# One-core attention and expert kernel: column-block matmuls, and another order of work behind the last scores

## What is computed

```python
Q, K, V = x @ wq, x @ wk, x @ wv                    # 16 heads of 8
local = window_attention(Q, K, V)                   # window of 32 rows
GQ = x @ wgq; GK, GV = pool8(x @ wgk), pool8(x @ wgv)   # 8 latent heads of 8, 64 latents a sequence
rem = (causal softmax(GQ GK^T) GV) @ r_out_w
att = (sigmoid(Q . gate_local_w) * local + sigmoid(Q . gate_remote_w) * rem) @ w_out
x = layernorm(x + att)
h = int(x[:, 0] + x[:, 1]) mod 8                    # experts h and h + 1 (mod 8), each weighted 1/2
y = sum over the two experts of 0.5 * (relu(x @ W1[e] + b1[e]) @ W2[e] + b2[e])
out = layernorm(x + y)
```

## Time and profile before

| | |
|---|---|
| median of 3 runs | 242.28 us (241.79 to 242.59) |
| profiled execution, its own time | 243.42 us |
| its span in the trace | 241.4 us |
| TensorE busy | 216.1 us, 90% |
| VectorE busy | 151.5 us, 63% |
| ScalarE busy | 121.5 us, 50% |
| POOL busy | 117.3 us, 49% |
| granted TensorE clock, mean | 0.958 of 2.4 GHz |

### The profile page before, as it was taken

How to read it: one execution, slowest core, us unless ns; L and a number is a source line. 1 busy time by engine, 2 the same in 40 slices (tenths; PEclk the granted TensorE clock), 3 DMA queues, 4 the chain that set the end, 5 groups by cost and what they waited for, 6 DMA issues and landing times.

```text
span 241.4 us, 9967 instructions
## 1 busy us (share of the span) xinstructions
PE 216.1 (90%) x3623; PEld 182.5 (76%) x3623; DVE 151.5 (63%) x523; ACT 121.5 (50%) x360; POOL 117.3 (49%) x218
## 2 busy tenths in 40 slices
PE   7979998999999999998996899897999999999930
PEld 3545777877888678886874599886899999999920
DVE  7835457795877867888898525374556656555640
ACT  3534656665577646765754246652434353434410
POOL 6453034661744428662747330648465465545541
PEclk9988999999999999999999569999999999999995
DMA  3231130032212233120001435412112112111100
GB/s 98 57 93 45 48 91 3 3 92 90 89 33 80 72 101 92 45 69 15 27 25 44 124 110 175 133 35 66 45 49 49 54 51 55 30 38 44 34 22 7
DMA packets 18553, 14.68 MB, mean 61 GB/s; under 512 B 2646, under 2 KB 15546, under 8 KB 18512
## 3 DMA queue, kind: packets, MB, share of 16 engines
q1 hardware_dynamic: 17008, 11.83, 17.5%
q0 software_dynamic: 1216, 2.16, 2.7%
q10 hardware_dynamic: 288, 0.13, 0.2%
HBM read 11.43 MB, written 3.03 MB: 60 GB/s over the span
## 4 chain that ended last, share of the span: by engine, by line
PE 64%; DVE 11%; issue 9%; DMA 6%; ACT 3%; POOL 2%; DVEq 2%; POOLq 1%; ACTq 0%
PE bS L1295 9%; PE bT L1244 7%; DMA out<-yo,idx 5%; PE bV L1435 4%; PE bV L1428 4%; PE bS L1187 4%; PE bV L1259 3%; PE bS L1212 3%; PE bV L1266 3%; PE bJ L1163 3%; PE bS L1226 2%; PE bL L1347 2%; PE bT L1295 2%; PE bS L1194 2%; PE bL L1361 2%
## 5 line engine op out<-in xcount | busy, mean ns | idle before, releaser
L681 ACT ACTIVATE ha<-bS,b1c 128x128 f32<-128x128 f32 x68 | 19.4, 368 | 40.0 <-PE bS L1295 40.0
L669 ACT COPY PTs<-bT 128x512 f32<-128x512 f32 (+3 forms) x48 | 25.8, 538 | 19.4 <-PE bT L1244 19.3
L568 POOL DMA_INDIRECT out<-yo,idx x18 | 19.2, 1067 | 17.8 <-POOL idx L564 9.8
L1244 PE MATMUL bT<-ident,Pr 128*128 128x128 f32 x168 | 27.4, 282 | 0.1
L1295 PE MATMUL bS<-xsT,w_s 128*128 128x128 f32 x204 | 26.4, 279 | 0.9 <-issue 0.8
L499 POOL TENSOR_SCALAR rstd<-mv 128x1 f32<-128x1 f32 x16 | 3.8, 235 | 45.7 <-DVE mv L860 45.7
L1295 PEld LDWEIGHTS bS<-xsT,w_s 128*128 128x128 f32 x204 | 24.1, 192 | 2.1 <-issue 2.1
L1244 PEld LDWEIGHTS bT<-ident,Pr 128*128 128x128 f32 x168 | 20.5, 147 | 4.1 <-issue 3.8
L515 POOL DMA_INDIRECT groups<-x,pos x16 | 16.6, 1035 | 12.5 <-DVE pos L910 9.1
L815 DVE TENSOR_REDUCE mx<-bS 128x8 bf16<-128x512 f32 x32 | 21.4, 676 | 0.0
L656 ACT ACTIVATE Pr<-bS 128x512 f32<-128x512 f32 x32 | 19.9, 622 | 2.6 <-PE bS L1226 2.6
(11 more groups left out here) (236 smaller groups left out, 515.5 us busy)
## 6 DMA issues: line engine op xcount, KB each, us to landing
w_s<-in_L_ffn_W SPq DMA_DIRECT2D x16, 256.0 KB
w1f<-in_L_ffn_W SPq DMA_DIRECT2D x10, 256.0 KB, 2.7
xrow<-groups SPq DMA_DIRECT2D x22, 64.5 KB, 1.8
xs<-groups SPq DMA_DIRECT2D x18, 64.0 KB
x_tok<-in_L_attn_x SPq DMA_DIRECT2D x4, 256.0 KB, 3.2
groups<-padrows SPq DMA_DIRECT2D x1, 516.0 KB, 5.7
b2r<-in_L_ffn_b SPq DMA_DIRECT2D x1, 512.0 KB, 3.7
out<-yo,idx POOLq DMA_INDIRECT x18
```

Source lines behind the costliest of these rows:

```text
L568: nc.gpsimd.indirect_dma_start(rows_out, bass.IndirectOffsetOnAxis(ap=idx[:], axis=0), yo[:, FULL - 1, :], None, bounds_check=T * P - 1, o ...
L669: nc.scalar.copy(PTs[:, j, 0:m, :], bT[:, 0:m * P].rearrange("p (c q) -> p c q", c=m)).then_inc(turned_out, 1)
L681: nc.scalar.activation(dst[:, c, :], src[:, c * P:(c + 1) * P], ACT.Relu, bias=bias_of(c)).then_inc(relu, 1)
L1244: last = nc.tensor.transpose(bT[:, c * P:(c + 1) * P], Pr[:, t % 2, j, c * P:(c + 1) * P], ident[:])
```

## The change

VectorE: residual(t - 3) moves ahead of the tile table in round T, and full_biases behind gate. The table loses two instructions (two steps made one by a constant that POOL prepares at the start; one cast for both rows of full_table), and a third (taken) moves behind the last mark. The five registers are read in three places: two ahead of gate(15), two ahead of residual(15), one behind the last mark. TensorE: weigh's latent part and fill "G" go by blocks of 32 weight columns into the four (for wgk two) quarters of the partitions; columns(0) moves from round T + 1 to the head of round T + 2; rank_last moves from j = 1, behind up_full(2, 0), to j = 0, behind up_full(1, 1). SyncE: one semaphore for each weight buffer instead of one for all, so that a load no longer waits for the one before it; weights 1 and 2 are asked for right behind the rows of tiles 0 and 1. ScalarE copies half the partitions of GKs.

```diff
@@ constants on POOL
+                link(nc.gpsimd.tensor_scalar(tile_scale[:], efl[:, 0:E], -1.0 / P, 0.5 / P - 0.5, ALU.mult, ALU.add))
@@ SyncE
             def load_full_weights(j):
-                if j >= 1:
-                    sp.wait_ge(w1f_in, 32 * j)
                 if j >= WR:
                     sp.wait_ge(up_b, j - WR + 1)
                 for s in range(2):
                     sp.dma_start(w1f[:, j % WR, s, :].unsqueeze(1),
-                                 W1[bass.ds((experts[j] + s) % E, 1)].rearrange("e p f -> p e f")).then_inc(w1f_in, 16)
+                                 W1[bass.ds((experts[j] + s) % E, 1)].rearrange("e p f -> p e f")).then_inc(w1f_in[j % WR], 16)
...
                 sp.dma_start(xrow[:, j * XW:(j + 1) * XW], seg[bass.ds(rows[j], P), :]).then_inc(full_in[j], 16)
-            for j in range(1, FULL):
+                if 1 <= j + 1 < WR:
+                    experts += load_table(sp, full_table[:, 0, :], [j + 1], full_ok, E - 1)
+                    load_full_weights(j + 1)
+            for j in range(WR, FULL):
                 experts += load_table(sp, full_table[:, 0, :], [j], full_ok, E - 1)
-                if j < WR:
-                    load_full_weights(j)
-            for j in range(WR, FULL):
                 load_full_weights(j)
@@ ScalarE
-                    nc.scalar.mul(GKs[:, q, :], src[:, 0:NL], 1.0 / CH)
+                    nc.scalar.mul(GKs[0:LD, q, :], src[0:LD, 0:NL], 1.0 / CH)
@@ VectorE
-                link(nc.vector.tensor_tensor(m[:, Z + 1:], nextrow[:], efl[:, 0:E], ALU.subtract))
-                link(nc.vector.tensor_scalar(m[:, Z + 1:], m[:, Z + 1:], 1.0 / P, 0.5 / P - 0.5, ALU.mult, ALU.add))
+                link(nc.vector.scalar_tensor_tensor(m[:, Z + 1:], nextrow[:], 1.0 / P, tile_scale[:], ALU.mult, ALU.add))
...
+                return upto
+
+            def take_tiles(upto):
                 link(nc.vector.tensor_tensor(taken[:], upto[:, Z + 1:], upto[:, Z:Z + E], ALU.subtract))
-                return upto
...
-                link(nc.vector.tensor_copy(full_table[:, 0, :], expert_of[0:1, :]))
-                nc.vector.tensor_copy(full_table[:, 1, :], rowf[0:1, :]).then_inc(full_ok, 1)
+                nc.vector.tensor_copy(full_table[:], found[0:1, :, :]).then_inc(full_ok, 1)
@@ VectorE, the loop over t
+                if t < T:
+                    largest(t, 2)
+                    largest(t, 0)
+                if t == T + 2:
+                    experts += load_table(dve, full_table[:, 0, :], [2, 3], full_ok, E - 1)
+                if t >= 3:
+                    residual(t - 3)
                 if t == T:
                     upto = full_tiles()
                     full_rows(upto)
-                if t < T:
-                    largest(t, 2)
-                    largest(t, 0)
-                if t >= 3:
-                    residual(t - 3)
+                if t == T + 1:
+                    experts = load_table(dve, full_table[:, 0, :], [0, 1], full_ok, E - 1)
...
+                if 2 <= t < T + 2:
+                    gate(t - 2)
                 if t == T:
                     full_biases()
-                if 2 <= t < T + 2:
-                    gate(t - 2)
...
             mark(NB - 1)
+            take_tiles(upto)
+            experts += load_table(dve, full_table[:, 0, :], [4], full_ok, E - 1)
             place(NB - 1)
             count_tiles()
-
-            experts = load_table(dve, full_table[:, 0, :], range(FULL), full_ok, E - 1)
@@ TensorE, fill "G"
-                    mm(dst[:, 0:NL], wgk_s[:], xp[:, q, :], start=True, stop=True)
+                    for i in range(LD // W):
+                        mm(dst[i * W:(i + 1) * W, 0:NL], wgk_s[:, i * W:(i + 1) * W], xp[:, q, :], start=True, stop=True)
 
                     for m in range(KT_):
-                        last = mm(dst[:, NL + m * LD:NL + (m + 1) * LD],
-                           xph[:, m, :, :].rearrange("p h l -> p (h l)"), wgv_s[:], start=True, stop=True)
+                        for i in range(BLK):
+                            last = mm(dst[i * W:(i + 1) * W, NL + m * LD:NL + (m + 1) * LD],
+                                      xph[:, m, :, :].rearrange("p h l -> p (h l)")[:, i * W:(i + 1) * W], wgv_s[:],
+                                      start=True, stop=True)
@@ TensorE, weigh, j == 2
                     for c in range(k + 1):
-                        last = mm(bV[:, HP * PW:(HP + LP) * PW], PTs[:, j, c, :],
-                                  GVx[:, b % 2, c, :, :].rearrange("p a w -> p (a w)"), start=(c == 0), stop=(c == k))
+                        for i in range(BLK):
+                            last = mm(bV[i * W:(i + 1) * W, HP * PW:(HP + LP) * PW], PTs[:, j, c, i * W:(i + 1) * W],
+                                      GVx[:, b % 2, c, :, :].rearrange("p a w -> p (a w)"), start=(c == 0),
+                                      stop=(c == k), skip_group_check=True)
@@ TensorE, up_full
-                    pe.wait_ge(w1f_in, 32 * (j + 1))
+                    pe.wait_ge(w1f_in[j % WR], 32 * (j // WR + 1))
@@ TensorE, the loop over t
                 if t == T + 2:
+                    columns(0)
                     up_full(0, 0)
...
-                if t == T + 1:
-                    columns(0)
@@ TensorE, the loop over full tiles
-                if j == 1:
-                    rank_last()
                 if j == 3:
                     more_tiles([2, 3])
                 down_full(j, 1)
                 if j + 1 < FULL:
                     up_full(j + 1, 1)
+                if j == 0:
+                    rank_last()
```

More of the change, by code:

```diff
@@ L141, in bass_windowed_latent_attention_hash_moe @@
         reached = sb("reached", [P, FULL, E])
-        expert_of = sb("expert_of", [P, FULL])
         cover = sb("cover", [P, FULL, E])
         gone = sb("gone", [P, FULL])
-        rowf = sb("rowf", [P, FULL])
         chosen = sb("chosen", [P, FULL, E])
@@ L150, in bass_windowed_latent_attention_hash_moe @@
         full_table = sb("full_table", [1, 2, FULL], I32)
+        tile_scale = sb("tile_scale", [P, E])
+        found = sb("found", [P, 2, FULL])
         w1_s = sb("w1_s", [P, E, F])
@@ L231, in bass_windowed_latent_attention_hash_moe @@
         scattered_late = sem("scattered_late")
-        w1f_in = sem("w1f_in")
+        w1f_in = [sem(f"w1f_in{j}") for j in range(WR)]
         full_ok = sem("full_ok")
@@ L937, in full_rows @@
                                              jrow[:, 0, :].unsqueeze(2).to_broadcast([P, FULL, E]), ALU.is_le))
-                nc.vector.tensor_reduce(expert_of[:], reached[:], AX.X, ALU.add)
+                nc.vector.tensor_reduce(found[:, 0, :], reached[:], AX.X, ALU.add)
                 link(nc.vector.tensor_tensor(cover[:], reached[:], ends, ALU.mult))
                 link(nc.vector.tensor_reduce(gone[:], cover[:], AX.X, ALU.max))
-                link(nc.vector.scalar_tensor_tensor(rowf[:], gone[:], -float(P), jrow[:, 1, :], ALU.mult, ALU.add))
-                link(nc.vector.scalar_tensor_tensor(rowf[:], expert_of[:], float(SEG), rowf[:], ALU.mult, ALU.add))
-                link(nc.vector.tensor_copy(full_table[:, 0, :], expert_of[0:1, :]))
-                nc.vector.tensor_copy(full_table[:, 1, :], rowf[0:1, :]).then_inc(full_ok, 1)
+                link(nc.vector.scalar_tensor_tensor(found[:, 1, :], gone[:], -float(P), jrow[:, 1, :], ALU.mult, ALU.add))
+                link(nc.vector.scalar_tensor_tensor(found[:, 1, :], found[:, 0, :], float(SEG), found[:, 1, :],
+                                                    ALU.mult, ALU.add))
+                nc.vector.tensor_copy(full_table[:], found[0:1, :, :]).then_inc(full_ok, 1)
             def full_biases():
                 dve.wait_ge(b1d_ok, 1)
-                link(nc.vector.tensor_tensor(chosen[:], expert_of[:].unsqueeze(2).to_broadcast([P, FULL, E]),
+                link(nc.vector.tensor_tensor(chosen[:], found[:, 0, :].unsqueeze(2).to_broadcast([P, FULL, E]),
                                              efl[:, 2 * E:].unsqueeze(1).to_broadcast([P, FULL, E]), ALU.is_equal))
```

## The result

The changed kernel takes 241.89 us (median of 20 runs, 239.09 to 245.10); the kernel before, beside it on the same chip, 243.32 us (20 runs, 241.79 to 244.66). The ratio is 0.9921, with a 95% interval of 0.9896 to 0.9947: faster by 0.8%, 1.4 us by the medians and 1.9 us by the ratio. The prediction asked for 5.35 us and its range ended at 239.6, so it was wrong. The profiled execution is a lucky one, at 239.59 us with a span of 237.9: 2.3 us under its own median, where that of before stood 1.14 over the median of the three runs known then and 0.10 over that of the 20. The two spans differ by 3.5 us, about twice what the change is worth.

What follows compares the result with a forecast made beforehand. The prediction took the chain as nearly two thirds TensorE, with VectorE stretches and late stores. Its terms, 2.5 + 1.0 - 0.75 + 0.6 + 2.0 = 5.35 us, came off 242.28 for 236.9 us, range 235.0 to 239.6.

Steps and rivals of the forecast that it cites:

- Part 1: Attention tiles: 32-column blocks in weigh latent and fill G shorten TensorE's groups, 2.5 us gain, bounds 0.5 to 3.5.
- (a): Attention tiles: VectorE's maxima and ScalarE's exponentials are the cycle, so column blocks give only 0.5 us, 238.9 us; chance 0.17.
- Parts 2 and 3: Behind the last scores: residual ahead of the table, columns(0) one step later; wO ends 1.0 us earlier, bounds 0 to 2.9.
- Part 4: Before the small tiles: rank_last one tile earlier makes TensorE stand for the ranks, -0.75 us; place comes 1.6 us earlier.
- Part 5: SyncE's weight loads: a semaphore for each buffer means weight 3 no longer comes late, 0.6 us gain.
- Part 6: First small expert tiles: VectorE's earlier register reads bring sums and stores forward, hb stall goes; 2.0 us, bounds 0 to 2.65.
- (b): Behind the last scores: the gains are eaten, all but the column blocks give 0.8 us together, 239.0 us; chance 0.13.
- (c): From 134 to 142 us: TensorE keeps 2.4 GHz, 1.9 us more gain, 235.0 us; chance 0.10.
- (d): Column blocks: 32-column weight loads don't overlap, so the kernel gets slower, 22 us slower at 0.11 us a load; chance 0.03.

Runs made afterwards that it cites:

- after: The changed kernel, with column blocks and new order, against the kernel before: 241.89 us, ratio 0.9921.
- blocks_only: The kernel before with the 32-column blocks alone (weigh latent, fill G, GKs copy): 243.13 us, ratio 1.0009 to the kernel before.
- order_gblocks: The changed kernel with only fill G's column blocks kept, weigh's latent part undone: 250.63 us on a slower chip, ratio 1.0101 to the kernel before.
- o_columns_back: The changed kernel without column blocks and with columns(0) back in round T + 1: 239.46 us, ratio 0.9842 to the kernel before.
- order_only: The changed kernel with the column blocks undone (full 128-column weights again): 239.31 us, ratio 0.9851 to the kernel before.
- o_weights_back: The changed kernel without column blocks and with SyncE's old order and waits for rows and weights: 239.55 us, ratio 0.9837 to the kernel before.
- before: The kernel without the change, run beside the others: 243.32 us beside the changed kernel, 242.86 to 249.27 us in the follow-up batches.
- before_spread: The kernel before with each round's second expert weight load (W2) sent half a round later: 242.77 us, ratio 0.9982 to the kernel before.
- o_regs_back: The changed kernel without column blocks and with VectorE's five register reads back in one piece: 240.53 us, ratio 0.9911 to the kernel before.
- o_rank_back: The changed kernel without column blocks and with rank_last back at j = 1: 238.60 us, ratio 0.9783 to the kernel before.
- after_spread: The changed kernel with each round's second expert weight load (W2) sent half a round later: 240.57 us, ratio 0.9877 to the kernel before.
- before_again: The kernel before, unchanged, run for a second trace on a slower chip: 247.95 us.
- after_again: The changed kernel, unchanged, run for a second trace on a slower chip: 247.81 us.
- after2: The changed kernel, unchanged, run again on a fourth, slow chip: 246.51 us, ratio 0.9888 to the kernel before.
- order_only2: The changed kernel without column blocks, run again on a fourth, slow chip: 247.87 us, ratio 0.9994 to the kernel before.

## Why the prediction was wrong, step by step

**Part 1, column blocks: 2.5 us forecast, none in the runs. This is the step that failed.** The prices were near in sum: a latent pass takes 0.51 / 24 = 0.021 us and not 0.016, so a latent block gains some 0.05 us ((0.85 - 0.64) / 4) and not 0.085, and a G gains 0.55 and not 0.45. The same count, 20 blocks and four Gs, comes to 3.2 us by these, against 3.5. What failed is "what TensorE saves there arrives, as long as VectorE and ScalarE keep up". It has two faults. First, less is saved than the count says: TensorE is busy only 1.1 us less, some 1.5 us arrive in traces with equal stalls, and 0.97 of 1.8 between tiles 4 and 12. Rival (a) had looked for this loss in VectorE's and ScalarE's pace. It is there once, as the 0.50 us behind the second G, but their waits don't grow in sum, and where the rest goes stays open.

The second fault is in no rival: TensorE's idle time grows by 1.4 us, and its "issue" stalls go from 1.26 to 3.17 us. The change adds 344 matmuls to TensorE's program, and the instruction stream is itself loaded, three transfers more (30 against 27). That the stalls are late instructions, the traces bear out; that the added matmuls make more of them is argued from `after` and `blocks_only` and not shown, since kernels without blocks had stalls of 1.01 and 0.99 us and `order_gblocks` had the most. The trace of before had such stalls in plain sight, 0.65, 0.19 and 0.23 us in TensorE's groups at 37.95, 52.21 and 67.67 us, if only as a small part of the 9% "issue" of the chain; I never asked what they were. What makes the runs of 242 to 245 us, of which no trace exists, is not shown either. Their mean granted clock is lower (0.950 in the two slowest, 0.970 and 0.973 in the two fastest), as in the longer runs of before, and whether a stall or the clock comes first can't be told without their traces.

**Parts 2 and 3, 1.0 us forecast, 0.1 to 0.3 in the traces.** With the lead of 1.33 us added, the table came at 132.6 us (132.6 forecast), SyncE asked for xrow(0) at 135.4 (135.4 forecast), columns(0) began at 137.7 (137.4) and up_full(0, 0) at 138.6 (138.0). Two terms were too small. xrow(0) needed 2.25 us to land behind two weight loads and not the median of 1.8, and the transpose, the copy and the hand-overs took 0.9 us and not 0.6. And at the low clock (0.55 and 0.60 from 136 to 144 us) the two up groups with aT between and wO needed 4.4 us and not 4.2. What the earlier trace rows showed as 1.56 us idle was slack of the last tile's chain for the most part: the next residual took its place with 1.18 us. `o_columns_back` shows no gain of part 3.

**Part 4, -0.75 forecast.** TensorE stands 0.23 us there in `order_only`; the stage is 0.4 to 0.5 shorter without the move, and the runs on the 243 us chips lean the same way (0.9783 against 0.9851, on different chips), those on the slow one the other (1.0003 against 0.9968, with intervals that overlap). Sign right on the one sort of chip, size some 0.5, and the gain it was made for stays unproved.

**Part 5, 0.6 forecast, 0 in the stage and 0.2 in the runs.** The weight is no longer late, but the 0.86 us wait of `o_weights_back` does not lengthen the stage. The ranks' wait and the clock hide it in that trace, so the worth of this part stays open.

**Part 6, 2.0 forecast, 1.9 to 2.04.** Right in its sum, a little late in its steps: measured from the first small tile, the wait for the fourth store ends 5.79 us behind it and not 7.37, where 2.3 us were to be gained and 1.6 were. The 1.23 us wait for hb is gone, and 0.73 us are left for ysum at 167.22 (0.6 forecast). The registers alone are 1.0 to 1.1 of it in the stage and 1.2 in the runs. No run takes the rest apart; the earlier start of place and scatter is my guess.

Parts 2 to 6 together were to give 2.85 us. `order_only` gave 3.6 by its ratio on one chip and 0.1 to 0.8 us on the slow one, and 2.3 in its trace on the first. So their sum came about right there, but nearly all that a trace shows of it is part 6; parts 2 to 5 were to give 0.85 and give next to nothing.

**The rivals.** (b) was wrong on the first chip: parts 2 to 5 lost their gain where it looked, but with part 6 they gave 2.3 us in the traces and not 0.8. On the slow chips it describes what came. (c) did not come: the clock fell later (1.00 in 132 to 136 us, where it was 0.54) and stayed low up to wO. (d) is false: 32-column weights with all 128 rows follow each other at 0.021 us a pass. The rule of the Trainium skill (TensorE: Matmul & The Clock Gate, "Packing small matmuls — row/col tiling") that the row group must differ for a load to overlap isn't what these rows show.

**The starting point.** I took the sum off the median of three runs, 242.28 us, where 20 gave 243.32, and read it from a profile of before at the low clock from 16 to 20 us. That belongs to the execution, not to the kernel, and made the comparison of two profiles look 1.5 us better than the runs.

## What to carry to other kernels

Cutting matmuls into more, smaller ones may be paid for in instructions: before counting on it, sum TensorE's idle time with "issue" as its releaser and see whether groups are cut in their middle near large transfers. Take a wait from one trace as a price only after asking what is late next; of four such waits here only one gave a gain that can be told, the registers in front of the sums, and that was 1.2 us where 1.7 to 2 were expected. And align two traces at a landmark ahead of the change before their spans are compared.

## What the runs showed of the hardware

- TensorE's "issue" stalls of 0.15 us or more between 20 and 130 us end 1.2 to 1.6 us behind an instruction transfer, in all 41 cases on the chips where before takes 243 us. Beside two loads of 256 KB they reach 1.94 us, behind 4 MB 3.47 us; with the DMA engines nearly idle there are stalls too, up to 2.57 us.
- In the stretch from 16 to 20 us the granted clock is 0.57 in the profiles of `before`, `before_spread`, `o_regs_back` and `o_weights_back` and 1.00 in `after`, `order_only`, `blocks_only`, `o_rank_back`, `o_columns_back`, `after_spread` and `before_again`, the last the same program as the first. The changed kernel has both sorts too: 0.57 in `after_again` and 0.50 in `after2`, the same program as `after`. It costs some 1.5 us. TensorE is busy throughout in both; why it falls stays open. The runs of before may hold both sorts.
- One program takes 243 us on some chips and 248 on others. On those, `before_again` and `order_only2` have the same set of cuts (0.3 to 0.55 us each, from 116 to 136 us) with the DMA engines nearly idle. They sum to some 3 us; what makes them is open.
- The order of parts 2 to 6 gains 1.5% on the one sort of chip and next to nothing on the other. The difference is more than any single part of it is worth.
